# Layer 0's keys: normed and weighted as rows, then turned by a DMA as pairs of 16-bit floats instead of by TensorE

## The reference

```python
kv = concatenate([context, layernorm(x)], axis=1)        # 128 + 128 rows
q, k, v = layernorm(x) @ Wq, kv @ Wk, kv @ Wv
q = q * rsqrt(mean(q*q) + 1e-6) * q_norm_w               # per head
k = k * rsqrt(mean(k*k) + 1e-6) * k_norm_w
scores = einsum('bhgqd,bhkd->bhgqk', q, k) / sqrt(128)   # 4 query heads share a key head
x = x + tanh(gate) * (softmax(scores) @ v) @ Wo
```

## Time and profile before

| | us |
|---|---|
| three runs, median (lowest to highest) | 1298.91 (1296.97 to 1300.86) |
| profiled execution, its own time | 1300.87 |
| its span in the profile | 1299.0 |
| granted TensorE clock, mean | 0.996 |

### The profile page before, as it was taken

The page is one execution under the profiler, slowest core; times in us unless marked ns, Lnnn a source line. Parts: engine busy times, 40 slices in busy tenths (PEclk is TensorE's granted clock), DMA queues, the critical chain, the costliest instruction groups (busy, mean ns, idle before and its releaser), DMA issues.

```text
span 1299.0 us, 24089 instructions
## 1 busy us (share of the span) xinstructions
PE 1267.6 (98%) x7520; PEld 1111.0 (86%) x7520; DVE 942.1 (73%) x2233; ACT 810.8 (62%) x2865; POOL 603.7 (46%) x959
## 2 busy tenths in 40 slices
PE   8899999999999999999999999999999999999998
PEld 6788888888888888888888888889989899778886
DVE  6778777777776786777777888877777778853434
ACT  5677676776777777677776664566666666622221
POOL 4656665665665666566567442323333323440000
PEclk9899999999999999999999999999999999999999
DMA  6464454444444453543545333243442334370000
GB/s 203 82 128 95 84 115 93 82 112 90 103 101 89 95 116 74 120 103 66 122 98 97 74 69 46 47 85 62 106 86 61 89 65 103 65 174 1 33 1 33
DMA packets 304259, 112.56 MB, mean 87 GB/s; under 512 B 272544, under 2 KB 290464, under 8 KB 304160
## 3 DMA queue, kind: packets, MB, share of 16 engines
q1 hardware_dynamic: 279072, 76.06, 30.9%
q10 hardware_dynamic: 21104, 29.12, 7.5%
q0 software_dynamic: 3984, 6.29, 2.0%
HBM read 39.08 MB, written 2.10 MB: 32 GB/s over the span
## 4 chain that ended last, share of the span: by engine, by line
PE 77%; DVE 9%; ACT 6%; issue 3%; POOL 3%; DMA 1%; DVEq 0%; SPq 0%; ACTq 0%; POOLq 0%
PE bank L524 21%; PE bank L526 21%; PE bank L525 21%; PE bank L753 7%; PE bank L771 4%; DVE split L1128 4%; ACT scratch L874 1%; PE bank L604 1%; ACT split L807 1%; DVE nb L1210 1%; DVE pieces L1228 1%; ACT pieces L886 1%; PE bank L612 1%; ACT bank L841 1%; POOL split L1467 1%
## 5 line engine op out<-in xcount | busy, mean ns | idle before, releaser
L524 PE MATMUL bank<-split 128*128 128x256 f32 (+6 forms) x2120 | 707.1, 334 | 13.6 <-DVE split L1128 5.6
L526 PE MATMUL bank<-split 128*128 128x256 f32 (+6 forms) x2120 | 692.6, 327 | 0.0
L525 PE MATMUL bank<-split 128*128 128x256 f32 (+6 forms) x2120 | 692.3, 327 | 0.0
L524 PEld LDWEIGHTS bank<-split 128*128 128x128 f32 (+2 forms) x2120 | 402.7, 190 | 57.1 <-DVE split L1128 12.2
L526 PEld LDWEIGHTS bank<-split 128*128 128x128 f32 (+2 forms) x2120 | 402.2, 190 | 35.2 <-issue 0.2
L525 PEld LDWEIGHTS bank<-split 128*128 128x128 f32 (+2 forms) x2120 | 403.1, 190 | 28.9
L1494 POOL CAST split<-turned 128x512 fp32r<-128x512 f16 x384 | 227.6, 622 | 284.0 <-DMA turned<-pieces 282.8
L874 ACT ACTIVATE scratch<-bank,nb 128x256 f32<-128x256 f32 x384 | 177.6, 474 | 111.6 <-DVE nb L1210 111.5
L1228 DVE SCALAR_TENSOR_TENSOR pieces<-scratch,rs,pieces 128x256 f16<-128x256 f32 x384 | 208.3, 583 | 10.0 <-ACT pieces L886 6.1
L807 ACT ACTIVATE split<-bank 96x256 fp32r<-96x256 f32 (+5 forms) x392 | 164.0, 429 | 81.7 <-PE bank L612 42.2
L1128 DVE TENSOR_TENSOR split<-bank,split 96x256 fp32r<-96x256 f32 (+5 forms) x392 | 185.0, 474 | 34.5 <-ACT split L807 27.4
(11 more groups left out here) (70 smaller groups left out, 1040.0 us busy)
## 6 DMA issues: line engine op xcount, KB each, us to landing
raw<-in_wq_a ACTq DMA_DIRECT2D x14, 512.0 KB, 4.1
raw<-in_wo_a ACTq DMA_DIRECT2D x14, 512.0 KB, 3.7
raw<-in_wkv_a ACTq DMA_DIRECT2D x7, 512.0 KB, 4.3
turned<-pieces SPq DMA_TRANSPOSE x192, 3.2
raw<-in_wq_c ACTq DMA_DIRECT2D x8, 384.0 KB, 3.4
craw<-in_ctx_t SPq DMA_DIRECT2D x8, 256.0 KB, 3.0
raw<-in_wo_c ACTq DMA_DIRECT2D x4, 512.0 KB, 3.6
split<-in_down_t POOLq DMA_DIRECT2D x2, 1024.0 KB, 5.7
```

What stands on the lines that cost most here:

```text
L524: pe.matmul(out, whi, mhi, start=start, stop=False)
L525: pe.matmul(out, whi, mlo, start=False, stop=False)
L526: return pe.matmul(out, wlo, mhi, start=False, stop=stop)
```

## The change

The product of the two norm weights is made as a row, broadcast over the partitions, and divided by its largest magnitude; the normed k is multiplied by it on DVE while it lies as rows. ACT writes the high 16-bit float, DVE the rest, SP issues one transposing DMA per tile, POOL casts the result. TensorE's two transposes per tile are gone in layer 0 (layer 1 keeps them). The factor that was divided out comes back as the scale of the exponential, so the negated maximum is multiplied by it too, in an instruction of its own. The halves and the turned k lie in what was `raw_kv`, so layer 0's k and v weights (and layer 1's first) are fetched into the second half of `raw_o`; that half's own fetch then waits for them to be split.

```diff
+        k_halves = raw[:, 2048:2304].bitcast(F16)
+        k_piece = chunks(k_halves, 2)
+        k_turned = raw[:, 2304:2560].bitcast(F16).rearrange("p (n q) -> p n q", q=P)
+        k_weight, q_weight = raw[:, 2560:2688], raw[:, 2688:2816]
+        k_squares = raw[:, 2816:3072]
+
+        def raw_kv_at(L, g):
+
+
+            return raw_o[:, 1024:2048] if L is L0 or (isinstance(g, int) and g == 0) else raw_kv
+
...
-                sp.dma_start(qkw[:, n:n + 1], a[name].rearrange("(p a) -> p a", a=1)).then_inc(in_small, 16)
+                sp.dma_start((q_weight, k_weight)[n], a[name].partition_broadcast(P)).then_inc(in_small, 16)
...
+            def turn_k(n):
+
+                s = attn[L0.name]
+                sp.wait_ge(s.kb_done, n + 1)
+                if n >= 1:
+                    sp.wait_ge(s.kcast_done, 2 * n)
+                sp.dma_start_transpose(k_turned, k_halves).then_inc(s.kturned, 16)
+
...
             turn_q(0)
+            turn_k(0)
             sp.wait_ge(in_x_rest, 16)
             sp.dma_start(xt[:, NB:NT, :], x_src[:, NB:NT, :]).then_inc(in_x_rest, 16)
+            sp.wait_ge(attn[L0.name].wkv_lo, 2)
             load_o(sp, L0, 0, 0)
             load_o(sp, L0, 0, 1)
             turn_q(1)
+            turn_k(1)
             next_context(4)
             for n in range(L0.tiles):
+                if 1 <= n < L0.tiles - 1:
+                    turn_k(n + 1)
                 turn(L0, n)
...
-                if starts(g, b - 1) and L is L0:
-                    pass
-                elif b > 0 or not isinstance(g, int) or g > 0:
+                if L is L0:
+                    if is_at(L, g, L0, 0) and b == 2:
+                        pe.wait_ge(s.kn_done, 2)
+                    elif not starts(g, b) and not starts(g, b - 1):
+                        pe.wait_ge(s.kn_done, count(g, b, 2, 0))
+                elif starts(g, b):
+                    pe.wait_ge(attn[L0.name].kn_done, 2 * L0.tiles)
+                else:
                     pe.wait_ge(s.klo_done, count(g, b, 1, 0))
-                elif L is L1:
...
-                pe.wait_ge(s.klo_done, count(g, b, 1, 1))
                 if L is L0:
+                    pe.wait_ge(s.kcast_done, count(g, b, 2, 2))
                     pe.wait_ge(s.qcast_done, count(g, b, 2, 2))
                 else:
+                    pe.wait_ge(s.klo_done, count(g, b, 1, 1))
...
-                if two is not None:
+                if two is not None and two[0] is L1:
                     k_turn(*two)
...
+            def k_high(L, g, b):
+
+                s = attn[L.name]
+                act.wait_ge(s.kn_done, count(g, b, 2, 2))
+                if not starts(g, b):
+                    act.wait_ge(s.kturned, count(g, b, 16, 0))
+                copy(k_piece[:, 0, :], kn).then_inc(s.ka_done, 1)
...
-                                   bias=nb[:, h:h + 1],
+                                   bias=nb[:, h:h + 1], scale=w_max[:, 2:3] if L.normed else 1.0,
...
+                if two is not None and two[0] is L0:
+                    k_high(*two)
...
-                        dve.tensor_scalar(out, k_rows, kr[:, 2 * (b % 2) + i:2 * (b % 2) + i + 1], None,
-                                          ALU.mult).then_inc(s.kn_done, 1)
+                        dve.scalar_tensor_tensor(out, k_rows, kr[:, 2 * (b % 2) + i:2 * (b % 2) + i + 1], k_weight,
+                                                 ALU.mult, ALU.mult).then_inc(s.kn_done, 1)
...
+                    dve.wait_ge(s.ka_done, count(g, b, 1, 1))
+                    dve.tensor_tensor(k_piece[:, 1, :], kn, k_piece[:, 0, :], ALU.subtract).then_inc(s.kb_done, 1)
...
+                pr = slice(2 * i, 2 * i + 2)
+                if L.normed:
+                    dve.tensor_reduce(mx[:, pr], chunks(bank[i][:, :], 2), AX.X, ALU.max, negate=True
+                                      ).then_inc(s.mx_done, 1)
+                    dve.wait_ge(s.mx_done, count(g, b, 2, i + 1))
+                    dve.tensor_scalar(nb[:, pr], mx[:, pr], w_max[:, 2:3], None, ALU.mult).then_inc(s.nb_done, 1)
+                else:
+                    dve.tensor_reduce(nb[:, pr], chunks(bank[i][:, :], 2), AX.X, ALU.max, negate=True
+                                      ).then_inc(s.nb_done, 1)
...
+            dve.tensor_tensor(k_weight, q_weight, k_weight, ALU.mult).then_inc(scalars, 1)
             dve.wait_ge(scalars, 1)
+            dve.scalar_tensor_tensor(q_weight, k_weight, -1.0, k_weight, ALU.mult, ALU.max).then_inc(scalars, 1)
+            dve.wait_ge(scalars, 2)
+            dve.tensor_reduce(w_max[:, 0:1], q_weight, AX.X, ALU.max).then_inc(scalars, 1)
+            dve.wait_ge(scalars, 3)
+            dve.tensor_scalar(w_max[:, 0:1], w_max[:, 0:1], 1e-30, None, ALU.max).then_inc(scalars, 1)
+            dve.wait_ge(scalars, 4)
+            dve.reciprocal(w_max[:, 1:2], w_max[:, 0:1]).then_inc(scalars, 1)
+            dve.tensor_scalar(w_max[:, 2:3], w_max[:, 0:1], float(L0.hd) ** 0.5 / QSCALE / QSCALE, None, ALU.mult
+                              ).then_inc(scalars, 1)
+            dve.wait_ge(scalars, 6)
+            dve.tensor_scalar(k_weight, k_weight, w_max[:, 1:2], QSCALE, ALU.mult, ALU.mult).then_inc(scalars, 1)
+            dve.wait_ge(scalars, 7)
...
+            def cast_k(L, g, b):
+
+                s = attn[L.name]
+                n = g * NT + b
+                pool.wait_ge(s.kturned, 16 * (n + 1))
+                if n >= 2:
+                    pool.wait_ge(s.s_done, 2 * (n - 1))
+                for c in range(2):
+                    pool.tensor_copy(kT[n % 2][c][:, 0, :], k_turned[:, 2 * c:2 * c + 2, :].rearrange("p n q -> p (n q)")
+                                     ).then_inc(s.kcast_done, 1)
...
                     q_norm(*three)
+                if two is not None and two[0] is L0:
+                    cast_k(*two)
```

More of the change, by code:

```diff
@@ L84, in __init__ @@
                 sem(n) for n in ("qa_done", "qb_done", "qturned", "qcast_done"))
+            self.ka_done, self.kb_done, self.kturned, self.kcast_done, self.mx_done = (
+                sem(n) for n in ("ka_done", "kb_done", "kturned", "kcast_done", "mx_done"))
         else:
@@ L87, in __init__ @@
                 sem(n) for n in ("qcp_done", "qt_done", "qthi_done", "qlo_done"))
+            self.kt_done, self.khi_done, self.klo_done = (sem(n) for n in ("kt_done", "khi_done", "klo_done"))
         self.in_q = sem("in_q")
@@ L603, in k_turn @@
                 for i in range(2):
-                    last = pe.transpose(kv_bank(L, g, b)[0:L.hd, i * P:(i + 1) * P], kn[:, i * L.hd:(i + 1) * L.hd],
+                    last = pe.transpose(bank[7][0:L.hd, i * P:(i + 1) * P], kn[:, i * L.hd:(i + 1) * L.hd],
                                         ident[:, :])
@@ L722, in _ @@
             q_proj(L0, 0, 1)
-            k_turn(L0, 0, 0)
             norm_turn(0, 2)
@@ L727, in _ @@
             q_proj(L0, 0, 2)
-            k_turn(L0, 0, 1)
             norm_turn(0, 3)
@@ L823, in kv_evac @@
                     for i in range(2):
-                        act.activation(kn[:, i * hd:(i + 1) * hd], ps[:, i * L.kvw:i * L.kvw + hd], ACT.Square,
+                        act.activation(k_squares[:, i * hd:(i + 1) * hd], ps[:, i * L.kvw:i * L.kvw + hd], ACT.Square,
                                        accum_out=ksum[:, 2 * (b % 2) + i:2 * (b % 2) + i + 1]
@@ L858, in k_evac @@
                 act.wait_ge(s.kt_done, count(g, b, 1, 1))
-                out, ps = kT[b % 2][0][0:L.hd, 0, :], kv_bank(L, g, b)[0:L.hd, 0:KV]
-                if L.normed:
-                    act.activation(out, ps, ACT.Copy, scale=qkw[:, 2:3]).then_inc(s.khi_done, 1)
-                else:
-                    copy(out, ps).then_inc(s.khi_done, 1)
+                copy(kT[b % 2][0][0:L.hd, 0, :], bank[7][0:L.hd, 0:KV]).then_inc(s.khi_done, 1)
+            def k_high(L, g, b):
[4 more added lines that the diff above has]
+                copy(k_piece[:, 0, :], kn).then_inc(s.ka_done, 1)
             def qt_evac(L, g, b):
@@ L901, in kv_hi @@
                 sl = slice(i * 2 * L.kvw, (i + 1) * 2 * L.kvw)
-                copy(flat(wkv[0])[:, sl], raw_kv[:, sl]).then_inc(s.wkv_hi, 1)
+                copy(flat(wkv[0])[:, sl], raw_kv_at(L, g)[:, sl]).then_inc(s.wkv_hi, 1)
             def q_hi(L, g, k):
@@ L917, in lora_weight_hi @@
                 copy(flat(lw[0]), raw_q[:, 0:KC * LW]).then_inc(lw_hi, 1)
-                copy(flat(lb[0]), raw_kv[:, 0:D]).then_inc(lw_hi, 1)
+                copy(flat(lb[0]), raw_q[:, KC * LW:KC * LW + D]).then_inc(lw_hi, 1)
             def lora_act_hi(t):
@@ L981, in step @@
                 if three is not None and three[0] is L0:
-                    if two is not None:
-                        k_evac(*two)
                     if one is not None:
@@ L1049, in load_next @@
                 if b == 4:
-                    act.wait_ge(s.wkv_lo, g * 2 + 2)
+                    if raw_kv_at(nl, ng) is not raw_kv:
```

(19 more changed lines are left out.)

42 lines of the change are left out of this document (17 added, 25 removed).

## The result

The changed kernel takes 1329.3 us (median of 4, 1325.9 to 1337.2) against 1299.1 before: ratio 1.0242, 95% interval 1.0194 to 1.029. The forecast was 1287. The profiled execution took 1328.57 us, span 1326.8.

The account below looks back on a forecast made before the run. TensorE, busy 98% of the span, was taken to bound the kernel. The terms -14.7 - 0.8 + 4.8 + 1 - 2 gave -11.7 us: 1289.2 from the profiled 1300.87, 1287 on the median; range 1277 to 1299.

Parts of the forecast that it names:

- the margin is 1.4 us, so a plain step waits for nothing: Plain step of layer 0: k's casts end at 409.3, the scores want k at 410.66; no wait, no cost.
- the 0.9 us of the scaling: Products of negated maxima on DVE (0.56) and scaled exponentials on ACT (0.32 per tile): k delayed by at most 0.9 us.
- `k_turn`: TensorE in layer 0: dropping its transposes saves 0.23 us per tile, 14.7 us over 64 tiles.
- Landing of k: k's transposing DMA in the loop: lands 3.2 us after its start, the median for the probabilities' turns.
- SP's slot: SP's queue: k's turn is issued before the probabilities are ready for theirs; no cost was put on it.
- The step with k and v weights: Step where POOL splits k and v weights: k about 0.7 us late in 8 groups, +4.8 us (0 to 21.6).
- The last group: Last group of layer 0, beside norms and experts: DVE in TensorE's way at some steps, +1 us (0 to 4.5).
- The start: Start of layer 0: `k_low` waits and perhaps the half clock go, -2 us (7 gained to 5 lost).
- k late in every tile: Rival: the scores wait for k's casts; at a 5.2 us landing k is 0.6 late in 64 tiles, 1325 us; chance 0.10.
- k late only beside weight fetches: Rival: in five of eight tiles k lands in 4.9 us, 0.3 late, 12 us in all, 1299 us; chance 0.13.
- all hidden: Rival: all of k hidden and the start clean, without the 4.8 and with 7 gained at the start, 1277; chance 0.15.
- this hold: DVE's two-SBUF-operand subtraction beside POOL's weight splits: 1.38 and 1.50 us instead of 0.47, counted for the k and v weights' step.

Follow-up runs that it names:

- x1: Changed kernel with the second half of the next group's output weights asked for one step later (step 7, not 6): 1310.0 us, ratio 1.0083.
- x4b: x1 without the product of the row maxima and without the exponential's scale, so it computes other numbers: 1295.5 us, ratio 0.9972.
- x7: Kernel before, plus the product of the row maxima and the exponential's scale, both from a column of ones: 1314.5 us, ratio 1.0116.
- x10: Kernel before, plus only the exponential's scale from a column of ones, without the product of the row maxima: 1301.7 us, ratio 1.0022.
- x5: Changed kernel without the 64 transposes of k; POOL casts k's rows unturned, so outputs are other numbers: 1304.4 us, ratio 1.0039.
- x3: Changed kernel with k put behind the first half of the probabilities in every queue (DVE, SP, POOL): 1350.6 us, ratio 1.039.
- x9: x1 with a fixed power of two (2^3) in place of the maximum, its product and the exponential's scale: 1298.8 us, ratio 0.9996.
- x2: Kernel before, with the second half of the next group's output weights asked for sooner, at the end of step 5: 1304.5 us, ratio 1.0045.

## Why the prediction was wrong

**The failed step** is "the margin is 1.4 us, so a plain step waits for nothing", taken as the answer for all steps of the loop but that of the k and v weights, with the 0.9 us of the scaling hidden in it, and with the second half of the probabilities not followed at all. The runs showed 19.3 us of collision on that second half in step 6 and 11.2 to 14.6 us of scaling instead. The plain step itself came as foretold. Here is POOL's timeline (L1591 casts k, L1552 the first half), to set beside the earlier trace rows; the scores start at 410.46, 2.87 us after `kv_proj`, and POOL stands for 1.20 us before its next work. This step follows a long step 6, so k has more room here (its casts end 2.6 us before the scores) than in the other plain steps of groups 2 and 3 (0.7 to 1.8 us, about the margin of the prediction):

```profile
407.12 0.74 POOL L1591 CAST split<-raw 128x256 fp32r<-128x256 f16 x2
409.00 1.17 POOL L1552 CAST split<-turned 128x512 fp32r<-128x512 f16 x2 [1.13 <-DMA turned<-pieces]
411.37 0.20 POOL L1559 TENSOR_TENSOR kvar<-ksum,hd_eps 128x2 f32<-128x2 f32 x1 [1.20 <-ACT raw L851]
```

But three of eight steps had no such margin. The term was well sized (2 x 0.35 + 4 x 0.09 = 1.05 us for 0.9) and misplaced: a plain step is 11.14 with it and without. Of the 16.7 us between the profiles of x1 and x4b, 9.4 lie in steps 1, 5 and 6, those with weights, and 3.4 in the last group. In the kernel before, the larger part of its price is that of the products on DVE (x7 against x10). And what was followed to its deadline was k and the first half of the probabilities; the second half, last of three turns, was followed nowhere. It met a fetch that is asked for 3.3 us into the step, before and after, however late the softmax is. That fetch stood in the code and in the trace.

**Point by point.** `k_turn`: foretold 0.23 us per tile, measured 0.26 in plain steps (404.36 in the earlier trace rows is the third matmul of `values` and not the second; the sum is right). Landing of k: foretold 3.2 from the earlier trace rows, measured 2.4 in the median:

```profile
turned<-scratch SPq DMA_TRANSPOSE x64, 3.8
raw<-raw SPq DMA_TRANSPOSE x64, 2.4
```

SP's slot: the half-sized turn holds SP as long as a full one (1.19 against 1.24 us), which the sum did not price ahead of the probabilities: in plain steps it ends up to 0.4 us after their first half is written. x5 shows what that slot does in step 6. The step with k and v weights (+4.8 foretold, from k being 0.7 late at the scores of step 6): the scores waited 0.1 to 0.3 us for k there, 1.3 in all in groups 1 to 6. k left some 0.5 us later in the step than put, but landed in 2.4 us and not 3.2. Step 5 itself grew by 2.1, through the probabilities:

```profile
296.70 0.50 PE L549 MATMUL bank<-split 128*128 128x512 f32 x1 [0.47 <-POOL split L1552]
```

The last group: +1 foretold, +2.6 measured, in step 2, where TensorE waited 3.3 us for the rows of a norm (L1189). The start: -2 foretold, +0.6 measured up to step 1 of group 0; the half clock did not go, 10.2 us of it (from 35.1 and 48.8 us on) in place of 6.8.

**Rivals.** "k late in every tile" gave 1325, near the measured time, and did not happen: plain steps of groups 1 to 6 show no wait for k. x3, with k's turn 1 to 3 us later in the step, shows that wait in four of eight steps. "k late only beside weight fetches" had the right place and the wrong victim. The case "all hidden" is the pace of the plain steps alone.

The Trainium skill (SBUF — State Buffer, "Who interferes with whom") was weighed for `k_low` in the step of POOL's splits: an instruction of VectorE with two SBUF inputs contends with one of GpSimd that reads SBUF. The trace after agrees with it, 1.39 us there against 0.42 in a plain step:

```profile
285.13 0.42 DVE L1223 TENSOR_TENSOR raw<-scratch,raw 128x256 f16<-128x256 f32 x1
...
299.54 1.39 DVE L1223 TENSOR_TENSOR raw<-scratch,raw 128x256 f16<-128x256 f32 x1
```

POOL split weights at that time:

```profile
298.11 2.54 POOL L1525 TENSOR_TENSOR split<-raw,split 128x512 fp32r<-128x512 f32 x2
```

The held instruction stands ahead of the probabilities' rest on DVE, so it has a part in the 2.1 us by which the second half came later in its step; how large a part no run shows. The prediction counted this hold in step 5 alone. It stands in step 1 as well, where POOL splits the output weights (1.40 us in groups 1 to 7).

The other rule of the Trainium skill, that one turn of a 128x128 block belongs on TensorE if PSUM will do (VectorE: DVE Perf Modes, "Rules for kernel authors"), is not spoken against here. By DMA, without scaling and collision, k gains nothing (x9), though not because its latency is seen in a plain step.

## What to carry to other kernels

Follow every transfer that is issued behind the new one to its deadline, in each kind of step, and look at what other queue it meets then: a step that works out in a plain stretch says nothing of the steps with weights. A small product on an engine that goes from one late thing to the next without a pause costs about its length there (two of 0.5 and 0.2 us on DVE made step 5 of x7 0.6 us longer than that of x10), whatever the engine's idle time over the span. If a latency is moved towards a bulk transfer, move that transfer too, and test this first: it was one line.

## What the runs showed of the hardware

- Turns and a 512 KB fetch in another queue shared the 16 DMA engines (54.6 and 43.3%), and in step 6 of the changed kernel the turn landed just behind the fetch: 4.8 to 7.0 us in place of 3.1. How much lead a turn needs is not one number here: 0.95 us sufficed in x5 (landing in 3.4 us), 0.99 did not in x2 (5.0). That stays open.
- A product with a per-partition factor on POOL took 927 ns where a copy of the same shape took 398. On ACT the exponential with a scale per partition took 562 ns, without 474.
- In four of the seven steps 6 of the changed kernel TensorE stood for 2.4 to 3.5 us, and the granted clock fell to half (1.2 GHz) for 3.4 or 6.8 us. A wait of 2.4 us in step 6 of group 4 came with a step 5.0 us longer than a plain one.
